# The output bias of an expert block: three pieces held in 3 rows, or in 128 rows of which 125 are zero

## The chip, the cores and the metric

The kernel runs on one core of a Trainium2 chip. The metric is the device time of one execution, in microseconds. The time before is 408.74 us, the median of three runs (407.4 to 409.92). Of the core's engines TensorE is called PE, VectorE DVE, ScalarE ACT, GpSimd POOL and SyncE SP. PE loads a stationary operand (a weight load, PEld in the profile) and then streams a moving operand through it (a matmul).

## What is computed

Sixteen sequences of 256 tokens with 128 features go through one layer: a layer norm, a causal linear attention with a residual, a second layer norm, and a mixture of 8 experts, of which each token takes the best two. Cut to what matters here:

```
x = x + attention(layernorm(x))
logits = layernorm(x) @ Wr + br                 # top 2 of 8 experts per token
h = relu(layernorm(x) @ W1[e] + b1[e])          # 128 -> 512
expert_out = h @ W2[e] + b2[e]                  # 512 -> 128, the bias b2 is the subject here
x = x + sum over the token's 2 experts of routed * expert_out
```

## The kernel before

**Stages.** Projections for the attention run until about 50 us, the attention with its prefix sums and the routing of tokens until about 240 us. During the routing POOL writes each token's normalised row to a table in HBM, `x_rows`, at a place that belongs to its expert (indirect DMAs, L468, two for each tile of 128 tokens). Then comes the stage of the experts: `NBLK` = 39 blocks of 256 places (`GPB` = 2 tiles of 128), each of one expert. Their results go back to `y_rows` in HBM by POOL's indirect DMAs (`scatter_y`, L500 to L506, two for a block). After the last one SP loads `y_rows`, ACT and DVE mix it into `x`, and SP stores the output.

**A block of experts.** The order is written out by hand, engine by engine (L1390 to L1395 for PE): at step n PE does `up(n+2)`, `down(n)`, `turn_block(n+4)`.
- `turn_block` (L1324): 4 matmuls of 128 columns turn the loaded rows around.
- `up` (L1342 to L1344): 12 matmuls of 256 columns, in fp16. Ahead of them PE's sequencer loads the block's expert number (L1332).
- `down`: first the matmul with the bias (L1364), 256 columns, then 16 matmuls of 128 columns (L1372, L1373) and 8 more (L1377), in fp16. Of the first 16, half use registers that the sequencer computes from the expert number just ahead of them.

**Around PE.** ACT copies the turned rows (L654), applies bias and relu (L669), and copies a block's result out of PSUM (L677) into one of 8 buffers (`YG`), from which POOL scatters it. DVE rounds the hidden values to fp16 (the cast, L1058) and makes the rest (L1062, a subtraction), one of each for a block. POOL's order, too, is by hand: two x scatters and then the two y scatters of block n for n = 0 to 5 (L515 to L518), then y scatters alone. SP loads block n's rows (L352). From block `N1` = 15 on this waits for all x scatters; its turn stands on PE after `down(11)`.

**The bias.** `b2` is split into three bf16 pieces, whose sum is the fp32 value. Each piece is a row of `b2p` (3 partitions, 8 experts x 128). The matmul at L1364 has `ones3` (3 x 128, all one) as its stationary operand and the expert's three rows of `b2p` as moving operand, so that it writes the sum of the pieces to every token's row. `ones3` is set by POOL at L395, `b2p` comes by a DMA of SP at L337. A second tile, `ones_b` (96 rows of ones, bf16, L373), is the stationary operand of the two bias matmuls of the projections (L1142, L1144).

Of the kernel before, what the change touches and what calls it, by code (L numbers as in the profile page):

```python
# [7 lines left out]
BF16 = mybir.dt.bfloat16  # L8
# [6 lines left out]
def block_kernel(nc, x_d, wqkv_d, bqkv_d, wproj_d, bproj_d, w1_d, b1_d, w2_d, b2_d, wr_d, br_d, out_d):  # L15

    P = 128
    SEQS, T, D = x_d.shape
    NT = SEQS * T // P
    U = SEQS  # L20
    TPU = T // P
    H, DH = 16, D // 16
    E, _, HID = w1_d.shape
    HC = HID // P
    LN_EPS, DEN_EPS = 1e-5, 1e-6
# [13 lines left out]
    B_ROWS = 96  # L39
# [3 lines left out]
    GPB = 2  # L43
# [34 lines left out]
    b2_parts = nc.dram_tensor("b2_parts", [3, E, D], BF16).ap()  # L78
    yv = y_rows[0:YROWS, :].rearrange("(p t c) d -> p t c d", p=P, c=TOP)

    with ExitStack() as ctx:
        def sb(name, shape, dt=F32):
            return ctx.enter_context(nc.sbuf_tensor(name, shape, dt))

        def sem(name):
            return ctx.enter_context(nc.semaphore(name))

        ps = ctx.enter_context(nc.psum_tensor("ps", [P, 8, 512], F32))
# [17 lines left out]
        bias_qk = sb("bias_qk", [B_ROWS, TPU, 2 * D], BF16)  # L106
        bias_v = sb("bias_v", [B_ROWS, TPU, D], BF16)
        bproj = sb("bproj", [P, D])
        ones_b = sb("ones_b", [B_ROWS, P], BF16)

        b1r = sb("b1r", [E * HC, P])
        b1T = sb("b1T", [P, E * HC])
        b1s = sb("b1s", [P, E * HC])
        b2hml = sb("b2hml", [E, 3, D], BF16)
        b2p = sb("b2p", [3, E, D], BF16)
        ones3 = sb("ones3", [3, P], BF16)
        ident = sb("ident", [P, P])
        tri = sb("tri", [P, P])
        ones = sb("ones", [P, P])
# [94 lines left out]
        late_done = sem("late_done")  # L214
# [28 lines left out]
        b2_in = sem("b2_in")  # L243
# [78 lines left out]
        @block.sync  # L322
        def _(sp):
            for g in range(LOADS):
                gt = slice(LN_TILES[g], LN_TILES[g + 1])
                sp.dma_start(x[:, gt, :], xv[:, gt, :]).then_inc(x_in[g], 16)
            sp.dma_start(wf[:, 0, :].rearrange("p (e h) -> p e h", e=E), w1_d.rearrange("e d h -> d e h")).then_inc(w1_in, 16)
            sp.dma_start(wf[:, 1, :].rearrange("p (e c d) -> p e c d", e=E, c=HC),
                         w2_d.rearrange("e (c p) d -> p e c d", p=P)).then_inc(w2_in, 16)
            sp.wait_ge(empty_done, 1)  # L330
            for e in range(E + 1):
                sp.dma_start(x_rows[e * REGION:e * REGION + SLOTS, :].rearrange("(p g) w -> p g w", g=GPB),
                             empty[:, :, :]).then_inc(empty_out, 16)
            sp.wait_ge(b2_done, 1)
            sp.dma_start(b2_parts.rearrange("r e d -> e r d"), b2hml[:, :, :]).then_inc(b2_in, 16)
            sp.wait_ge(b2_in, 16)
            sp.dma_start(b2p[:, :, :], b2_parts).then_inc(b2_in, 16)  # L337

            regs = [sp.alloc_register(name=f"row{j}") for j in range(XG)]
            for n in range(NBLK):  # L340
                b = n % XG
                if n in (0, N1):
                    i = 0 if n == 0 else 1
                    sp.wait_ge(table_done, 2 * (i + 1))
                    for c in range(TOP):
                        sp.wait_ge(x_scattered[i][c], 16 * (NT - T1 if i else T1))
                sp.load(regs[b:b + 1], table_i[0:1, 0, n:n + 1])
                row = sp.snap(regs[b], min_val=0, max_val=E * REGION)
                if n >= XG:
                    sp.wait_ge(turn_done, n - XG + 1)  # L350
                    sp.wait_ge(yid_done, n - XG + 1)
                sp.dma_start(xg_w[:, b, :], x_rows[bass.ds(row, SLOTS), :].rearrange("(p g) w -> p (g w)", g=GPB)  # L352
                             ).then_inc(loaded[b], 16)

            for b in range(YG):
                sp.wait_ge(y_scattered[b], 16 * GPB * len(range(b, NBLK, YG)))
            for g in range(Y_LOADS):
                gt = slice(g * TPY, (g + 1) * TPY)
                sp.dma_start(yg[:, gt], yv[:, gt]).then_inc(y_in[g], 16)
            for g in range(Y_LOADS):  # L360
                gt = slice(g * TPY, (g + 1) * TPY)
                sp.wait_ge(mix_done, g + 1)
                sp.dma_start(ov[:, gt, :], x[:, gt, :]).then_inc(out_done, 16)
            sp.wait_ge(out_done, 16 * Y_LOADS)

        @block.gpsimd
        def _(pool):
# [24 lines left out]
            layer_norm_1(1)  # L392
            layer_norm_1(2)
            nc.gpsimd.memset(empty[:, :, :], 0.0).then_inc(empty_done, 1)
            nc.gpsimd.memset(ones3[:], 1.0).then_inc(late_done, 1)  # L395
            nc.gpsimd.memset(ones_h[:], 1.0).then_inc(late_done, 1)
            nc.gpsimd.memset(picked[:, 0, :], 0.0).then_inc(late_done, 1)
            nc.gpsimd.iota(ints[:, 0:E], [[1, E]], base=0, channel_multiplier=0).then_inc(late_done, 1)
# [721 lines left out]
        def _(pe):  # L1120
# [15 lines left out]
            def qkv(u):  # L1136
                par = u % 2
                pe.wait_ge(xT_out, u + 1)
                if u >= 2:
                    pe.wait_ge(phi_done, u - 1)  # L1140
                    pe.wait_ge(v_done, u - 1)
                nc.tensor.matmul(ps[:, 2 + par, :], ones_b[:, :], bias_qk[:, :, :].rearrange("p a d -> p (a d)"),  # L1142
                                 start=True, stop=False)
                nc.tensor.matmul(ps[:, 4 + par, 0:T], ones_b[:, :], bias_v[:, :, :].rearrange("p a d -> p (a d)"),  # L1144
                                 start=True, stop=False)
                for a in range(TPU):
                    xT = xT_s[:, par, a * P:(a + 1) * P]
                    nc.tensor.matmul(ps[:, 2 + par, a * 2 * D:(a + 1) * 2 * D], xT, wqkv[:, 0:2 * D],  # L1148
                                     start=False, stop=(a == TPU - 1))
                    ins = nc.tensor.matmul(ps[:, 4 + par, a * D:(a + 1) * D], xT, wqkv[:, 2 * D:3 * D],  # L1150
                                           start=False, stop=(a == TPU - 1))
                ins.then_inc(qkv_done, 1)
# [140 lines left out]
            def spread(i):  # L1293

                n = (N1, N2)[i]
                pe.wait_ge(diag_done, 5 * (i + 1))
                nc.tensor.matmul(ps[:, 5 + i, (0, T)[i]:(0, T)[i] + 5 * n].rearrange("p (k n) -> p k n", k=5),
                                 ones[:, :], diag[:, :, 0:n], start=True, stop=True).then_inc(spread_done, 1)
# [49 lines left out]
            def down(n):  # L1348
                e = pe.snap(regs[n % 4], min_val=0, max_val=E - 1)
                if n >= 2:  # L1350
                    pe.wait_ge(y_out, n - 1)
                if n == 0:
                    pe.wait_ge(cnt_out, 2)
                if n == 1:
                    pe.wait_ge(rank_out, NG)
                if n == SPREAD - 1:
                    pe.wait_ge(y_out, n)
                if n == SPREAD:
                    pe.wait_ge(y_out, n)
                    spread(1)  # L1360
                if n == SPREAD + 2:
                    pe.wait_ge(table_done, 4)
                both = ps[:, 6 + n % 2, 0:GPB * D].rearrange("p (g d) -> p g d", g=GPB)
                nc.tensor.matmul(both, ones3[:, :], b2p[:, bass.ds(e, 1), :].broadcast_to([3, GPB, D]), start=True, stop=False)  # L1364
                outs = [ps[:, 6 + n % 2, g * D:(g + 1) * D] for g in range(GPB)]
                high = [(w2[:, bass.ds(e, 1), c, 0].rearrange("p a d -> p (a d)")) for c in range(HC)]
                low = [(w2[:, bass.ds(e, 1), c, 1].rearrange("p a d -> p (a d)")) for c in range(HC)]
                pe.wait_ge(hi_done, n + 1)
                for g, o in enumerate(outs):
                    for c in range(HC):  # L1370
                        h = hh[:, n % 2, c, g * P:(g + 1) * P]
                        nc.tensor.matmul(o, h, high[c], start=False, stop=False)  # L1372
                        nc.tensor.matmul(o, h, low[c], start=False, stop=False)  # L1373
                pe.wait_ge(lo_done, n + 1)
                for g, o in enumerate(outs):
                    for c in range(HC):
                        ins = nc.tensor.matmul(o, hl[:, n % 2, c, g * P:(g + 1) * P], high[c], start=False,  # L1377
                                               stop=(g == GPB - 1 and c == HC - 1))
                ins.then_inc(down_done, 1)
# [10 lines left out]
            for n in range(NBLK):  # L1390
                if n + 2 < NBLK:
                    up(n + 2)
                down(n)
                if n + 4 < NBLK:
                    turn_block(n + 4)  # L1395
# [23 lines left out]
```

## Time and profile before

| | |
|---|---|
| median of three runs | 408.74 us (407.4 to 409.92) |
| the profiled execution, its time | 409.99 us |
| its span, first to last instruction | 408.2 us |
| PE busy | 311.4 us, 2455 matmuls |
| PE weight loads | 240.3 us |
| DVE busy | 295.6 us |
| POOL busy | 279.7 us |
| ACT busy | 192.9 us |
| mean granted clock of PE | 0.889 |

The profiled execution took 1.8 us more than its span. Busy shares are means over stages that have different limits. A matmul's recorded time includes its way through the array, so matmuls that follow each other overlap in the records: what one costs is the distance from its start to the next start. In the timeline a number in brackets is the idle time of the engine before the row, with what ended it. "issue" means that nothing in the profile ended it.

### The profile page before, as it was taken

Reading aid. Unit: us, or ns where it says so; the run is one execution under the profiler, and the core shown is the slowest. Engines: PE = TensorE matmul, PEld = TensorE weight load, DVE = VectorE, ACT = ScalarE, POOL = GpSimd, SP = SyncE. Lnnn points to the kernel's source line nnn. Section 1 sums busy time; section 2 is a strip of 40 time slices with the busy share of each in tenths; the row PEclk is TensorE's granted clock in tenths of the full one; section 3 lists DMA queues with packets and bytes.
Section 4 is the critical chain, followed back from the end, with each engine's and each line's share of the span. In section 5 each row is a group of like instructions: output and inputs, shape, how many; then the busy total and the mean of one; then the engine's idle time right before and its main releaser. Section 6 shows DMA issues by size and latency. Waiting matters only on the chain.

```text
span 408.2 us, 8336 instructions
## 1 busy us (share of the span) xinstructions
PE 311.4 (76%) x2455; PEld 240.3 (59%) x2455; DVE 295.6 (72%) x707; ACT 192.9 (47%) x479; POOL 279.7 (69%) x249
## 2 busy tenths in 40 slices
PE   0799696986899895898942479999899999993000
PEld 0578464664676663575731347888788888883000
DVE  3988948777789899698993577777567776673067
ACT  2498306277521510513130436766677777762063
POOL 3479525899945888898667463788778788787600
PEclk9999988898999998998975559999999999999555
DMA  7990000000000000000011042221423322111198
GB/s 206 321 256 3 1 2 1 1 2 0 0 2 0 28 28 26 26 26 29 33 46 54 20 125 67 82 73 44 137 84 96 85 82 81 57 43 47 51 359 259
DMA packets 24064, 29.41 MB, mean 72 GB/s; under 512 B 3819, under 2 KB 18675, under 8 KB 24022
## 3 DMA queue, kind: packets, MB, share of 16 engines
q1 hardware_dynamic: 18582, 18.99, 15.5%
q0 software_dynamic: 4544, 9.38, 7.2%
q10 hardware_dynamic: 896, 0.50, 0.5%
q8 instruction: 23, 0.38, 0.4%
q14 instruction: 19, 0.16, 0.1%
HBM read 16.19 MB, written 12.67 MB: 71 GB/s over the span
## 4 chain that ended last, share of the span: by engine, by line
PE 28%; DVE 24%; issue 20%; POOL 14%; ACT 6%; DMA 5%; SPq 1%; POOLq 0%; DVEq 0%; ACTq 0%
POOL y_rows L504 12%; PE ps L1175 7%; DVE work L839 5%; DVE nd L845 4%; PE ps L1174 2%; DVE y_s L856 2%; DMA qk<-y_rows 2%; PE ps L1148 2%; DVE wm L747 2%; ACT xs L603 2%; POOL x_rows L468 2%; PE ps L1342 2%; PE ps L1343 2%; PE ps L1344 2%; PE ps L1372 2%
## 5 line engine op out<-in xcount | busy, mean ns | idle before, releaser
L504 POOL DMA_INDIRECT y_rows<-kvt,yid x78 | 95.4, 1223 | 30.4 <-issue 21.6
L438 POOL TENSOR_TENSOR kvt<-qk,v 128x1024 f32<-128x1024 f32 x32 | 67.5, 2133 | 29.7 <-PE ps L1179 18.9
L468 POOL DMA_INDIRECT x_rows<-rows,pos_i x64 | 66.0, 1031 | 30.5 <-issue 17.3
L1175 PE MATMUL ps<-kvt,tri 128*128 128x384 f32 (+1 forms) x192 | 72.9, 493 | 11.6 <-DVE work L839 11.6
L669 ACT ACTIVATE wraw<-ps,b1s 128x256 f32<-128x256 f32 x156 | 61.1, 474 | 3.1 <-PE ps L1344 2.5
L1175 PEld LDWEIGHTS ps<-kvt,tri 128*128 128x128 f32 x192 | 38.3, 206 | 33.2 <-issue 18.0
L1058 DVE CAST wraw<-wraw 128x1024 f16<-128x1024 f32 x39 | 27.3, 699 | 34.5 <-ACT wraw L669 33.3
L839 DVE TENSOR_TENSOR work<-ps,qk 128x1152 f32<-128x1152 f32 x32 | 42.2, 1350 | 11.0 <-PE ps L1179 10.7
L1062 DVE TENSOR_TENSOR wraw<-wraw 128x1024 f16<-128x1024 f32 x39 | 47.8, 1225 | 1.3
L1342 PE MATMUL ps<-wraw,w1h 128*128 128x256 f16 x156 | 43.7, 280 | 0.3 <-issue 0.3
L1343 PE MATMUL ps<-wraw,w1h 128*128 128x256 f16 x156 | 43.7, 280 | 0.0
L1344 PE MATMUL ps<-wraw,w1l 128*128 128x256 f16 x156 | 43.6, 279 | 0.0
L845 DVE TENSOR_REDUCE nd<-work 128x144 f32<-128x1152 f32 x32 | 41.6, 1341 | 0.0
L1372 PE MATMUL ps<-w,wraw 128*128 x312 | 40.6, 221 | 0.8 <-DVE wraw L1058 0.8
L1373 PE MATMUL ps<-w,wraw 128*128 x312 | 40.1, 219 | 0.0
L1174 PE MATMUL ps<-kvt,ones 128*128 128x384 f32 (+1 forms) x96 | 37.0, 467 | 0.0
L1372 PEld LDWEIGHTS ps<-w,wraw 128*128 128x128 f16 x312 | 29.5, 97 | 6.0 <-issue 1.3
L677 ACT ACTIVATE kvt<-ps 128x256 f32<-128x256 f32 x39 | 14.9, 383 | 35.3 <-PE ps L1377 35.3
L1373 PEld LDWEIGHTS ps<-w,wraw 128*128 128x128 f16 x312 | 30.4, 98 | 0.4
L654 ACT ACTIVATE wraw<-ps 128x512 f16<-128x512 f32 x39 | 23.1, 594 | 5.1 <-PE ps L1324 5.1
L588 ACT ACTIVATE xT_s<-ps 128x256 f32<-128x256 f32 x16 | 6.1, 383 | 40.3 <-PE ps L1186 40.3
L1377 PE MATMUL ps<-w,wraw 128*128 x312 | 23.8, 219 | 0.0
(211 smaller groups left out, 643.1 us busy)
## 6 DMA issues: line engine op xcount, KB each, us to landing
wraw<-x_rows SPq DMA_DIRECT2D x39, 130.0 KB, 2.3
qk<-y_rows SPq DMA_DIRECT2D x8, 512.0 KB, 6.5
wraw<-in_L_ffn_W_dram SPq DMA_DIRECT2D x1, 2048.0 KB, 12.7
out_dram<-x SPq DMA_DIRECT2D x8, 256.0 KB, 4.7
x<-in_L_attn_x_dram SPq DMA_DIRECT2D x3, 512.0 KB, 10.0
y_rows<-kvt,yid POOLq DMA_INDIRECT x78, 2.5
x_rows<-empty SPq DMA_DIRECT2D x9, 130.0 KB, 4.1
x_rows<-rows,pos_i POOLq DMA_INDIRECT x64, 2.3
```

What stands on the lines that cost most here:

```text
L438: nc.gpsimd.tensor_tensor(kvt[:, u % RING, a].rearrange("p (j h i) -> p j h i", j=DH, i=DH), k.unsqueeze(1).broadcast_to([P, DH, H, DH]), ...
L468: nc.gpsimd.indirect_dma_start(out=x_rows, out_offset=bass.IndirectOffsetOnAxis(ap=pos_i[:, c, t:t + 1], axis=0), in_=rows[:, t, :], in_of ...
L504: nc.gpsimd.indirect_dma_start(out=y_rows, in_=ysb[:, n % YG, g], in_offset=None, out_offset=bass.IndirectOffsetOnAxis(ap=yid[:, n, g:g + ...
L669: ins = nc.scalar.activation(hid[:, n % 2, c], ps[:, 2 + 2 * (n % 2) + c // 2, at:at + SLOTS], ACT.Relu, bias=b1s[:, bass.ds(e * HC + c, 1)])
L839: nc.vector.tensor_tensor(m_s[:, a].rearrange("p (b j n) -> p b j n", b=3, j=PLB), ps[:, 3 * a:3 * a + 3, 0:PLB * D].rearrange("p b (j n) ...
L845: nc.vector.tensor_reduce(nd[:, s % 2, a, :], m_s[:, a].rearrange("p (n i) -> p n i", i=DH), AX.X, ALU.add).then_inc(red_done, 1)
L1175: nc.tensor.matmul(o, tri[:, :], kv[a][:, cols], start=(a == 0), stop=True)
L1342: nc.tensor.matmul(o, wh, xh, start=True, stop=False)
L1343: nc.tensor.matmul(o, wh, xl, start=False, stop=False)
L1344: ins = nc.tensor.matmul(o, wl, xh, start=False, stop=True)
L1372: nc.tensor.matmul(o, h, high[c], start=False, stop=False)
L1373: nc.tensor.matmul(o, h, low[c], start=False, stop=False)
```

## The change

`ones_b` has 128 rows instead of 96. `ones3` is gone. `b2p` has 128 rows: POOL clears it, where it set `ones3` before, and SP's DMA then writes the pieces into rows 0 to 2, behind a wait for POOL's late constants. The bias matmul of a block takes all 128 rows of `ones_b` and of `b2p`. The bias matmuls of the projections take the first 96 rows of `ones_b`, as before.

```
-        ones_b = sb("ones_b", [B_ROWS, P], BF16)
+        ones_b = sb("ones_b", [P, P], BF16)
...
-        b2p = sb("b2p", [3, E, D], BF16)
-        ones3 = sb("ones3", [3, P], BF16)
+        b2p = sb("b2p", [P, E, D], BF16)
...
             sp.wait_ge(b2_in, 16)
-            sp.dma_start(b2p[:, :, :], b2_parts).then_inc(b2_in, 16)
+            sp.wait_ge(late_done, 16)
+            sp.dma_start(b2p[0:3, :, :], b2_parts).then_inc(b2_in, 16)
...
-            nc.gpsimd.memset(ones3[:], 1.0).then_inc(late_done, 1)
+            nc.gpsimd.memset(b2p[:, :, :], 0.0).then_inc(late_done, 1)
...
-                nc.tensor.matmul(both, ones3[:, :], b2p[:, bass.ds(e, 1), :].broadcast_to([3, GPB, D]), start=True, stop=False)
+                nc.tensor.matmul(both, ones_b[:, :], b2p[:, bass.ds(e, 1), :].broadcast_to([P, GPB, D]), start=True, stop=False)
```

No instruction is added, removed or moved on PE, ACT, DVE or SP. On POOL the order is the same as well, and two fills have another size. This is POOL's list at the constants that are set after the first layer norms; `empty` is the block of zeros with which `x_rows` is cleared.

```order
 L394 MEMSET empty 128x260
-L395 MEMSET ones 3x128
+L395 MEMSET b2p 128x1024
 L396 MEMSET ones_h 128x128
 L397 MEMSET picked 128x8
```

The fill at L395 has grown from 128 to 1024 elements in a partition, and stays in its place.

## Rows read from the trace of the kernel before

**Rows 1.** The page, chain of work that ended last, by line.
```profile
POOL y_rows L504 12%; PE ps L1175 7%; DVE work L839 5%; DVE nd L845 4%; PE ps L1174 2%; DVE y_s L856 2%; DMA qk<-y_rows 2%; PE ps L1148 2%; DVE wm L747 2%; ACT xs L603 2%; POOL x_rows L468 2%; PE ps L1342 2%; PE ps L1343 2%; PE ps L1344 2%; PE ps L1372 2%
```

**Rows 2.** Windows: stretch, length, busy us of PE, PEld, DVE, ACT, POOL, then clock.
```profile
310.00:362.00 52.00, 52.00 (x667) 44.82 (x665) 36.60 (x67) 38.12 (x99) 41.94 (x34) 1.00 0.26 75
362.00:386.00 24.00, 9.38 (x116) 7.42 (x114) 7.44 (x16) 6.24 (x17) 18.69 (x18) 0.79 0.15 47
```

**Rows 3.** Timeline of PE: start, duration, line, operation, tiles.
```profile
320.55 0.27 PE L1343 MATMUL ps<-wraw,w1h 128*128 128x256 f16 x1
320.66 0.27 PE L1344 MATMUL ps<-wraw,w1l 128*128 128x256 f16 x1
320.87 0.28 PE L1364 MATMUL ps<-b2p,ones 3*128 x1
321.08 0.23 PE L1372 MATMUL ps<-w,wraw 128*128 x1
321.14 0.22 PE L1373 MATMUL ps<-w,wraw 128*128 x1
```

**Rows 4.** Timeline of the weight loads (PEld), the same place.
```profile
320.86 0.09 PEld L1364 LDWEIGHTS ps<-b2p,ones 3*128 3x128 bf16 x1 [0.21 <-issue]
```

**Rows 5.** Line L1364 from 308 to 362: count, ns, first and last start; idle before.
```profile
L1364 PE MATMUL ps<-b2p,ones x17: 278/278/279, 308.1 to 359.1; 3*128 x17
...
  issue: 3.6, 17
```

**Rows 6.** Timeline of PE in the projections: 96 rows, bf16, then fp32.
```profile
17.71 0.27 PE L1144 MATMUL ps<-bias_v,ones_b 96*128 96x256 bf16 x1
17.82 0.60 PE L1148 MATMUL ps<-wqkv,xT_s 128*128 128x256 f32 x2
```

**Rows 7.** Timeline of PE in the routing: one row, then 128 rows, both fp16.
```profile
246.47 0.18 PE L1249 MATMUL ps<-base_h,ones_h 1*128 1x16 f16 x1
246.58 0.18 PE L1250 MATMUL ps<-picked,before_h 128*128 128x16 f16 x1
```

**Rows 8.** Line L1332 of PE's sequencer, from 286 to 290, and from 287 to 360.
```profile
L1332 PEldq TENSOR_LOAD <-table_i x2: 297/302/307, 286.9 to 289.8; - x2
...
L1332 PEldq TENSOR_LOAD <-table_i x24: 297/300/355, 286.9 to 359.9; - x24
```

**Rows 9.** Timelines of DVE and of POOL, a block in the middle.
```profile
324.99 0.69 DVE L1058 CAST wraw<-wraw 128x1024 f16<-128x1024 f32 x1 [0.91 <-ACT wraw L669]
325.72 1.23 DVE L1062 TENSOR_TENSOR wraw<-wraw 128x1024 f16<-128x1024 f32 x1
...
326.15 1.62 POOL L504 DMA_INDIRECT y_rows<-kvt,yid  x1 [0.31 <-issue]
328.08 0.96 POOL L504 DMA_INDIRECT y_rows<-kvt,yid  x1 [0.30 <-issue]
```

**Rows 10.** Timelines of DVE and of POOL, near the end of the blocks.
```profile
366.24 0.69 DVE L1058 CAST wraw<-wraw 128x1024 f16<-128x1024 f32 x1 [0.41 <-ACT wraw L669]
...
366.63 1.12 POOL L504 DMA_INDIRECT y_rows<-kvt,yid  x1 [0.30 <-issue]
```

**Rows 11.** Timeline of PE, the turn of block 15.
```profile
286.85 0.40 PE L1324 MATMUL ps<-ident_h,wraw 128*128 128x128 f16 x4 [1.19 <-DMA wraw<-x_rows]
```

**Rows 12.** Timeline of POOL, its last scatter.
```profile
384.91 0.96 POOL L504 DMA_INDIRECT y_rows<-kvt,yid  x1 [0.31 <-issue]
```

**Rows 13.** Timeline of POOL, two fills.
```profile
1.34 0.53 POOL L374 MEMSET bias_qk<- 96x512 bf16 x1
...
19.18 0.19 POOL L395 MEMSET ones<- 3x128 bf16 x1
```

**Rows 14.** Timelines of POOL and ACT, behind the constants.
```profile
24.36 0.20 POOL L389 TENSOR_TENSOR shift<-lnt,rstd 128x8 f32<-128x8 f32 x1
26.25 0.87 ACT L538 ACTIVATE work<-x,shift,rstd 128x128 f32<-128x128 f32 x2
28.78 1.66 POOL L387 TENSOR_TENSOR rstd<-lnt,neghalf 128x8 f32<-128x8 f32 x1 [1.89 <-DVE lnt L722]
```

More of the change, by code:

```diff
@@ L1141, in qkv @@
                     pe.wait_ge(v_done, u - 1)
-                nc.tensor.matmul(ps[:, 2 + par, :], ones_b[:, :], bias_qk[:, :, :].rearrange("p a d -> p (a d)"),
+                nc.tensor.matmul(ps[:, 2 + par, :], ones_b[0:B_ROWS, :], bias_qk[:, :, :].rearrange("p a d -> p (a d)"),
                                  start=True, stop=False)
-                nc.tensor.matmul(ps[:, 4 + par, 0:T], ones_b[:, :], bias_v[:, :, :].rearrange("p a d -> p (a d)"),
+                nc.tensor.matmul(ps[:, 4 + par, 0:T], ones_b[0:B_ROWS, :], bias_v[:, :, :].rearrange("p a d -> p (a d)"),
                                  start=True, stop=False)
```

## The prediction

> **What bounds the kernel now.** I read the chain that ended last first. Its largest entry is POOL's scatter of results, L504, with 12% of the span [rows 1]. Then I read the windows, to see which engine is full beside POOL: from 310 to 362 us PE is busy for all of 52.00 us, POOL for 41.94, ACT for 38.12 and DVE for 36.60 [rows 2]. So two engines could be the bound of the expert blocks: PE, which never rests, and POOL, which still has work when PE has none. In the next window PE is busy for 9.38 us and POOL for 18.69 [rows 2], and the last scatter starts at 384.91 [rows 12]. All that follows (loads, mixing, stores) hangs on that scatter. The reader should keep both in mind: a faster PE is worth something only if POOL becomes faster with it.
>
> The period of a block is (359.1 - 308.1) / 16 = 3.19 us [rows 5]. The sequencer's line gives the same over a longer stretch: (359.9 - 286.9) / 23 = 3.17 [rows 8].
>
> **What the bias matmul costs.** Two up matmuls of 256 columns start 0.11 us apart (320.55, 320.66). The bias matmul starts 0.21 after the last of them, and the first down matmul 0.21 after the bias (320.87, 321.08) [rows 3]. It has 256 columns as well, so that a matmul like its neighbours would take 0.11 on each side. The surplus is 0.10 + 0.10 = 0.20 us for a block. The weight load of the bias sits idle for 0.21 us ahead of it, with nothing in the profile that ended it [rows 4], and this is so at all 17 blocks of the stretch, 3.6 us in all [rows 5]; elsewhere in that window loads run beside matmuls (44.82 us of them under 52.00 us [rows 2]).
>
> Is it the three rows, or the bf16 among fp16? Two places tell them apart. In the projections a bias matmul of 96 rows in bf16 with 256 columns is followed by an fp32 matmul after 17.82 - 17.71 = 0.11 us [rows 6]: another type, many rows, no surplus. In the routing a matmul of one row and only 16 columns is followed by one of 128 rows, both fp16, after 0.11 us [rows 7], twice the 0.06 that separates two down matmuls of 128 columns [rows 3]: one type, few rows, and a surplus. So it goes with the rows. I expect 0.20 us less for a block; the bounds are 0 (the gaps stay) and 0.20 (nothing can be closer than its neighbours).
>
> A rule of the Trainium skill names such a mechanism: "TensorEngine Tiling (Array Packing)", section Tiling Modes, Key Properties, says that going from one tiling mode to another makes the array drain, and rows 3 fit it on both sides of the bias. By that rule the whole 0.20 us goes. A second page speaks against the change: "TensorE: Matmul & The Clock Gate", Part 3, has a weight load overlap matmuls in flight only where it targets another row group, which padding to 128 rows would take away. Rows 4 disagree: the small load is the one that doesn't overlap.
>
> **Does the sequencer keep up?** PE's period would be 3.19 - 0.20 = 2.99. Its sequencer also computes registers and loads an expert number. Right behind the stall of block 15 its queue is empty, and there it went from one block's load to the next in 289.8 - 286.9 = 2.9 us [rows 8]. That is one sample, read to a tenth. It is close enough to 2.99 that some blocks may be held up by it, so the gain per block is between 0.18 and 0.20, with 0.10 as a poor case.
>
> **Does POOL follow?** In steady state POOL does two scatters for a block: one of 1.62 and one of 0.96 us, each after 0.30 of idle: 1.62 + 0.96 + 0.60 = 3.18, PE's period [rows 9]. Alone they would take 2 x (0.96 + 0.30) = 2.52. The 0.66 us of the long one is either a fixed price of working beside DVE, or a wait for DVE. Its end tells: DVE's subtraction ends at 325.72 + 1.23 = 326.95, and the long scatter at 326.15 + 1.62 = 327.77, 0.82 later [rows 9]. Near the end, at another phase, a scatter is stretched by only 0.16 (1.12 instead of 0.96); DVE's cast ends at 366.24 + 0.69 = 366.93, and this scatter at 366.63 + 1.12 = 367.75, again 0.82 later [rows 10]. So a scatter that starts under one of DVE's two long operations waits for its end, and then takes 0.82. POOL is held in step by DVE, DVE by ACT, ACT by PE. DVE and ACT have room (36.60 and 38.12 of 52.00 [rows 2]).
>
> At a period of 2.99, measured from the end of the subtraction: scatter one ends at 0.82, scatter two starts at 1.12 (0.30 of idle). The cast now begins 2.99 - (0.69 + 1.23 + 0.04) = 1.03 and ends at 1.72; scatter two waits for it and ends at 2.54; scatter three starts at 2.84, under the subtraction, which ends at 2.99. The pattern closes, two scatters to a block, at any period above 2.52. So POOL's stretch shrinks by what PE's period does, and its backlog behind PE at the end stays as it is.
>
> **The other edits.** POOL's fill of 128 rows x 1024 bf16 in place of 3 x 128: 96 x 512 took 0.53, 3 x 128 took 0.19 [rows 13], (0.53 - 0.19) / (512 - 128) x (1024 - 128) = 0.8 us more; the bounds are 0 and twice that. It delays what stands behind it on POOL. The shift of the fourth group ends at 24.36 + 0.20 = 24.56 and ACT uses it at 26.25, 1.7 us later; before the fifth POOL waits 1.89 us for DVE [rows 14]. Both cover 0.8; without that cover it would be 0.8 us once. SP's new wait needs POOL's late constants, which DVE has waited for too (L915) before it made the pieces that this DMA carries: nothing. `ones_b` with 128 rows instead of 96 has the same elements in a partition: nothing.
>
> **The sum.** Blocks 0 to 11 gain 0.20 each on PE. Then PE waits 1.19 us for the load of block 15 [rows 11], which hangs on the last x scatter. POOL reaches that scatter in step with DVE, over some ten periods, so it comes about 10 x 0.20 = 2.0 us earlier, and the wait stays. Behind it blocks 12 to 36 gain 25 x 0.20 = 5.0. The last two blocks are bound by latencies. That is 7.0 us with 0.20, and 6.3 with 0.18. POOL may fall a step out of phase once, which costs up to one stretch of 0.66. I take 6.5 us. The profiled span would go from 408.2 to 401.7, its time from 409.99 to 403.5; the median of runs lay 1.25 below that execution, so the median goes from 408.74 to 402.2.
>
> **Rivals.**
> - *Both follow* (0.74): 402.2, its own range 401 to 403.8.
> - *Half of it* (0.08): only one of the two gaps closes, or the sequencer holds PE at about 3.09. 35 x 0.10 = 3.5 us, 405.2. For it: one sequencer sample near the limit. Against: the registers of L1364 are no more than before.
> - *POOL doesn't follow* (0.11): the 0.66 is a fixed price, or the gaps stay (the change does nothing, 0.03 of this). POOL needs 3.18 for a block as before, PE only gets further ahead until the 8 buffers are full: 408.7. Against it is the stretch of 0.16 in rows 10.
> - *Slower* (0.07): POOL's phase turns bad. If the cast falls on the middle of a scatter and the subtraction on the start of the next, both are stretched; taken as 0.16 more for the second than now [rows 10], over 35 blocks that is 5.6 us, 414.3, and with a full 0.66 twice it would be 23 us. It decides where the cast starts after scatter two has begun: 1.12 after the subtraction's end, that is at a period above 1.12 + 1.96 = 3.08; at today's 3.19 it starts 0.11 after, and its end just clears the end of the scatter. The shorter period moves away from that, hence the small chance.
> - Among the slower ones, 0.02: a load of 128 rows that has to wait for the matmuls ahead lies open with 0.09 us [rows 4] in 39 blocks, 3.5 us: 412.2. This is what the second page would make of it.
>
> **How the numbers follow.** About 1% (4.1 us) is what can be told from no change here, so faster means under 404.6. The first case lies wholly there: 0.74, and a part of the second, where the sequencer costs less than half, brings it to 0.76. The same: the rest of the second and the third, 0.17. Slower: 0.07. For eight in ten the range takes in the first case and the second: 400.6 (the full 7.0 us and 1.1 of scatter between medians) to 405.6.
>
> **What the new profile would show.** The bias matmul starts 0.11 after the last up matmul, and the first down matmul 0.11 after it; no idle time ahead of the load of L1364; a period of 2.99 to 3.01. POOL's scatters of a block take 0.96 and about 1.42, or two stretched ones with 0.46 between them. The wait before block 15's turn is still about 1.2. The last scatter starts near 378.4. If the gaps are gone and the last scatter still starts near 385, the step about POOL is wrong; if the gaps are there, the step about rows.

## The result and the profile after

The changed kernel takes 403.32 us (median of five runs, 401.13 to 406.1) where the kernel before takes 408.74 (five runs, 406.69 to 411.76). The ratio is 0.986, with an interval of 0.9814 to 0.9905: 5.4 us faster. The prediction was 402.2, with a range of 400.6 to 405.6.

| | before | after |
|---|---|---|
| median | 408.74 us | 403.32 us |
| profiled execution, its time | 409.99 us | 406.1 us |
| its span | 408.2 us | 404.3 us |
| PE weight loads, busy | 240.3 us | 245.7 us |
| POOL busy | 279.7 us | 275.6 us |
| L504, mean of a scatter | 1223 ns | 1169 ns |
| mean granted clock | 0.889 | 0.891 |

The profiled execution of after is the slowest of its five, so its span must be read with care. Below, the lengths of its stages are compared with those of before, and not only its end.

PE around the bias matmul, the place of [rows 3], as the timeline of after has it:

```profile
320.95 0.27 PE L1344 MATMUL ps<-wraw,w1l 128*128 128x256 f16 x1
321.06 0.27 PE L1364 MATMUL ps<-b2p,ones_b 128*128 x1
321.17 0.22 PE L1372 MATMUL ps<-w,wraw 128*128 x1
```

The bias matmul starts 0.11 us after the up matmul, and the first down matmul 0.11 after the bias. Both gaps of 0.21 are gone. The line L1364 over the window from 305 to 360 answers to [rows 5]:

```profile
L1364 PEld LDWEIGHTS ps<-b2p,ones_b x18: 97/98/98, 305.8 to 357.4; 128*128 128x128 bf16 x18
L1364 PE MATMUL ps<-b2p,ones_b x18: 272/272/273, 305.9 to 357.6; 128*128 x18
```

The 3.6 us of idle time ahead of its weight load, "issue", no longer stand there. The period is (357.6 - 305.9) / 17 = 3.04 us, where it was 3.19.

The windows of after (start and end, length, busy us of PE, PEld, DVE, ACT, POOL, then the granted clock, the DMA share and GB/s), the first two for [rows 2]:

```profile
310.00:362.00 52.00, 52.00 (x707) 48.91 (x705) 38.02 (x69) 39.90 (x103) 41.63 (x35) 1.00 0.27 80
362.00:386.00 24.00, 7.49 (x92) 6.22 (x89) 7.04 (x13) 4.68 (x13) 15.43 (x15) 0.75 0.21 65
...
251.90:380.80 128.90, 115.34 (x1517) 107.06 (x1514) 84.80 (x165) 86.12 (x222) 102.32 (x88) 0.96 0.26 77
```

In the same 52 us PE does 707 matmuls where it did 667. The third window is the most telling. It runs from POOL's first scatter of results to its last one. The same stretch of before is this:

```profile
250.90:384.90 134.00, 119.03 (x1517) 101.55 (x1514) 84.78 (x166) 86.30 (x222) 107.43 (x87) 0.97 0.25 74
```

DVE and ACT have the same busy time in both. POOL is busy for 107.43 us of 134.00 before, and for 102.32 of 128.90 after. What is left is 26.57 and 26.58: POOL has about 88 scatters in either window and idles 0.30 us ahead of each. In neither trace is any idle time ahead of a scatter in these windows longer than 0.31 us. So POOL works through the whole stage without a break in both kernels, and all of the 5.1 us comes out of the recorded duration of its scatters. None comes from idle waits. (A scatter's duration contains what it waits for DVE, as the part on why the prediction was right shows.)

### The profile page after: what moved, and what is told of

Read it like the earlier page. It is cut to its first block, busy times and chain, and to the rows that moved or that the text cites. A ratio compares the mean times of both kernels' runs of the same rounds, so it can differ in the third digit from the quotient of the medians.

```text
span 404.3 us, 8337 instructions
## 1 busy us (share of the span) xinstructions
PE 307.2 (76%) x2455; PEld 245.7 (61%) x2455; DVE 297.3 (74%) x707; ACT 192.9 (48%) x479; POOL 275.6 (68%) x249
## 4 chain that ended last, share of the span: by engine, by line
DVE 27%; POOL 22%; PE 20%; issue 16%; ACT 7%; DMA 5%; SPq 1%; POOLq 0%; ACTq 0%; DVEq 0%
POOL y_rows L504 18%; PE ps L1175 6%; DVE work L839 5%; DVE nd L845 4%; POOL x_rows L468 4%; DVE y_s L856 3%; DMA qk<-y_rows 3%; PE ps L1174 3%; PE ps L1148 2%; DVE wm L747 2%; ACT xs L603 2%; DMA x<-in_L_attn_x_dram 1%; DVE qk L742 1%; PE ps L1150 1%; DVE rd L853 1%
## 5 line engine op out<-in xcount | busy, mean ns | idle before, releaser
L504 POOL DMA_INDIRECT y_rows<-kvt,yid x78 | 91.2, 1169 | 30.3 <-issue 20.1
L1372 PE MATMUL ps<-w,wraw 128*128 x312 | 43.5, 222 | 1.1 <-DVE wraw L1058 1.0
L1373 PE MATMUL ps<-w,wraw 128*128 x312 | 43.3, 223 | 0.0
L1372 PEld LDWEIGHTS ps<-w,wraw 128*128 128x128 f16 x312 | 30.9, 99 | 2.7 <-issue 1.6
L1373 PEld LDWEIGHTS ps<-w,wraw 128*128 128x128 f16 x312 | 30.1, 99 | 1.9
L1377 PE MATMUL ps<-w,wraw 128*128 x312 | 24.0, 220 | 0.0
```

What stands on the lines that cost most here:

```text
L504: nc.gpsimd.indirect_dma_start(out=y_rows, in_=ysb[:, n % YG, g], in_offset=None, out_offset=bass.IndirectOffsetOnAxis(ap=yid[:, n, g:g + ...
```

## Experiments

Each experiment was made on one chip together with runs of the kernel before. There were four such sets. In two of them the kernel before took 408.92 and 408.59 us, as it did when its profile was taken; in the other two it took 424.32 and 428.37. Those two sets are read by themselves.

### Is it the rows, and from what size on?

Four kernels keep everything of the change (the larger fill, SP's wait, `ones_b`, the 128 rows of `b2p`) and give the matmul at L1364 fewer of the rows: 3, 32, 64 or 96. The rows left out are zero, so the result is the same.

```
-  matmul(both, ones_b[:, :], b2p[:, bass.ds(e, 1), :].broadcast_to([P, GPB, D]), ...)
+  matmul(both, ones_b[0:3, :], b2p[0:3, bass.ds(e, 1), :].broadcast_to([3, GPB, D]), ...)
```

> The changed kernel with the bias matmul of a block back on 3 rows of ones_b and 3 rows of b2p; the wider tiles, POOL's larger fill and SP's added wait stay. Theory (a matmul of few rows between matmuls of 128 rows costs about 0.10 us on each side, and nothing else in the change matters): the gaps of 0.21 us before and behind L1364 are back, the period is 3.19 us, the time is that of the kernel before, 408.7 us, ratio 0.997 to 1.003. Rival (part of the 5.4 us came from elsewhere, as from the layout of the tiles): under 407 us. Rival (the larger fill and the wait cost something): over 409.5 us.

> The bias matmul of a block with 32 rows, all zero but the three pieces. Theory 1 (the array has modes of 32, 64 and 128 rows, and going between them costs): as with 3 rows, first down matmul 0.21 us behind the bias, period 3.19. Theory 2 (the surplus grows smaller with each row that is added): gaps between 0.11 and 0.21.

> The bias matmul of a block with 64 rows. Theory 1 (modes of 32, 64 and 128 rows): 64 rows is another mode than 128, the gaps stay at 0.21 us and the period at 3.19. Theory 2 (only matmuls that fit into 32 rows are special): 0.11 us and a period of about 3.04.

> The bias matmul of a block with 96 rows, as the bias matmuls of the projections have. Theory 1 and 2 alike: 0.11 us on both sides and a period of 3.04, as with 128 rows, since 96 rows need all of the array's rows. If gaps are left, then it is not modes, and all 128 rows are needed.

The line L1364 in the window from 305 to 360, of the kernels with 3, 32, 64 and 96 rows (the idle time ahead of its weight load is shown for the first; with 96 rows there is none):

```profile
L1364 PE MATMUL ps<-b2p,ones_b x17: 278/278/278, 306.5 to 357.5; 3*128 x17
...
  issue: 3.6, 17
```

```profile
L1364 PE MATMUL ps<-b2p,ones_b x18: 278/278/279, 305.1 to 359.3; 32*128 x18
```

```profile
L1364 PE MATMUL ps<-b2p,ones_b x17: 279/279/280, 306.9 to 358.0; 64*128 x17
```

```profile
L1364 PE MATMUL ps<-b2p,ones_b x19: 274/274/275, 305.2 to 359.8; 96*128 x19
```

| rows of L1364 | gap ahead, behind | period | span | time |
|---|---|---|---|---|
| 3 | 0.20, 0.21 | 3.19 | 406.8 | 409.11, 10 runs, ratio to before 0.9999 (0.9968 to 1.0031) |
| 32 | 0.20, 0.21 | 3.19 | 409.4 | 411.28, one run |
| 64 | 0.20, 0.21 | 3.19 | 407.1 | 408.92, one run |
| 96 | 0.11, 0.11 | 3.03 | 403.4 | 405.21, one run |
| 128 (after) | 0.11, 0.11 | 3.04 | 404.3 (that execution took 406.1) | 403.32, median of five |

The periods are worked out as above, for 96 rows (359.8 - 305.2) / 18. The edge lies between 64 and 96 rows: with 3, 32 and 64 rows the price is the same, so it doesn't shrink with each row that is added. With 64 rows, half of the 128, the timeline shows both gaps:

```profile
322.66 0.27 PE L1344 MATMUL ps<-wraw,w1l 128*128 128x256 f16 x1
322.86 0.28 PE L1364 MATMUL ps<-b2p,ones_b 64*128 x1
323.07 0.23 PE L1372 MATMUL ps<-w,wraw 128*128 x1
```

The kernel with 3 rows has the whole of the change but this one number, and has the time of before. So the gain of the kernel after hangs on the rows of the matmul alone, and the larger fill and SP's wait cost nothing that shows. All five kernels have bf16 beside fp16, so the type alone makes no gap. The times of the single runs are worth less than the periods: where the stage of experts starts differs between executions. ACT's copy of block 0 starts at 250.6, 249.1 and 250.7 us with 32, 64 and 96 rows.

### Is the price one for a matmul, or for a change of size?

The kernel before, with its bias matmul issued twice in a row (the second adds the bias again).

```
   matmul(both, ones3[:, :], b2p[:, bass.ds(e, 1), :].broadcast_to([3, GPB, D]), start=True, stop=False)
+  matmul(both, ones3[:, :], b2p[:, bass.ds(e, 1), :].broadcast_to([3, GPB, D]), start=False, stop=False)
```

> The kernel before with the bias matmul of 3 rows issued twice in a row (the bias is added twice, so the output differs by b2). If the price is for each change between few rows and 128 rows: the second matmul starts 0.11 us behind the first, and the surplus of a block stays 0.20: 0.21 ahead, 0.11 between, 0.21 behind, a period of 3.30. If each matmul of few rows is slow by itself: 0.21 between the two, and a period of 3.40. The second matmul also needs a register, 0.12 us of the sequencer, which had room before.

```profile
331.38 0.27 PE L1344 MATMUL ps<-wraw,w1l 128*128 128x256 f16 x1
331.59 0.28 PE L1364 MATMUL ps<-b2p,ones 3*128 x1
331.71 0.27 PE L1365 MATMUL ps<-b2p,ones 3*128 x1
331.91 0.23 PE L1373 MATMUL ps<-w,wraw 128*128 x1
```

The distances are 0.21, 0.12 and 0.20. Between the two small matmuls there is nearly no surplus (0.12 where neighbours of 256 columns are 0.11 apart); it stands once on the way in and once on the way out. The period of 3.30 that was expected couldn't be tested, and the time of this run (425.60 us) says nothing, since its chip was one of those with another bound.

### Does the sequencer hold PE up?

The prediction had PE's period at 2.99 if only PE counts, and after shows 3.04. The timeline of after shows where the rest is. These are down matmuls of one block, all of 128 columns:

```profile
315.39 0.22 PE L1373 MATMUL ps<-w,wraw 128*128 x1
315.46 0.23 PE L1372 MATMUL ps<-w,wraw 128*128 x1
315.58 0.23 PE L1373 MATMUL ps<-w,wraw 128*128 x1
315.65 0.22 PE L1372 MATMUL ps<-w,wraw 128*128 x1
```

They start 0.06 us apart, but one comes after 0.12. From 310 to 357 us after has 9 such distances over 0.1 among the first 16 down matmuls of its blocks, and what these matmuls have above 0.056 adds up to 0.88 us, or 0.06 for each of some 15 blocks. A block without any takes 2.98 us, and 2.98 + 0.06 is the period of 3.04. Before has no distance over 0.1 there, nor has the kernel with 3 rows. All nine are ahead of the eighth of the 16, the last one whose register the sequencer computes just ahead. In the trace of after its computations for L1372 and L1373 (FUSED_REGOPS) start 0.124 us apart, as the two matmuls above do (315.46, 315.58), while PE by itself needs 0.056 for such a matmul. So the trace alone speaks for the sequencer; three experiments were to test it. The first lets the sequencer load two experts' numbers with one instruction, in every other block.

```
-                pe.load(regs[n % 4:n % 4 + 1], table_i[0:1, 1, n:n + 1])
+                at = (n + 1) % 4
+                if n == 0:
+                    pe.load(regs[at:at + 1], table_i[0:1, 1, n:n + 1])
+                elif n % 2 == 1:
+                    pe.load(regs[at:at + 2], table_i[0:1, 1, n:n + 2])
```

> The changed kernel, in which PE's sequencer loads the expert numbers of two blocks with one load (blocks 1 and 2, 3 and 4, and so on). A load and its wait took 0.36 us in the trace of after, so this frees 0.18 us of the sequencer for a block. Theory (the 0.05 us by which the period of after, 3.04, is over the 2.99 that PE's own matmuls need is the sequencer's): the period from block 16 on falls to 2.99 to 3.00, some 1.0 to 1.8 us off the time before x 0.987, about 401.8 us. Rival (the 0.05 is something else, as DVE or ACT): the period stays at 3.04 and the time at 403.3.

> The changed kernel with one load of expert numbers for two blocks, once more, since the first look ran on a chip on which the kernel before took 424 us and the blocks had another bound. If this chip takes 409 us for the kernel before: by the theory of the sequencer the period from block 16 on is 2.99 to 3.00 instead of 3.04, and the time about 402 us; by the rival 3.04 and 403.3. A load of two numbers took 0.60 us with its wait on the other chip instead of 0.36, so a block frees 0.06 us rather than 0.18, which just covers the 0.05. If it is a chip of 424 us again: as the kernel before.

On the chip where before took 424.32 this kernel took 424.53, a ratio of 0.9982 (0.9947 to 1.0017), no difference. On the chip where before took 408.59 it took 406.06 (ten runs), a ratio of 0.9957 (0.9929 to 0.9986): a little faster than before, yet behind the plain change (0.986, and 403.18 below on this same chip). Neither forecast came true, 402 us with a period of 2.99 or 403.3 with 3.04: the period from 310.5 to 354.3 us is 43.8 / 14 = 3.13. ACT's copies of the results show how it runs:

```profile
309.17 0.39 ACT L677 ACTIVATE kvt<-ps 128x256 f32<-128x256 f32 x1 [0.36 <-PE ps L1381]
312.45 0.38 ACT L677 ACTIVATE kvt<-ps 128x256 f32<-128x256 f32 x1 [0.94 <-PE ps L1381]
315.43 0.39 ACT L677 ACTIVATE kvt<-ps 128x256 f32<-128x256 f32 x1 [0.64 <-PE ps L1381]
318.78 0.38 ACT L677 ACTIVATE kvt<-ps 128x256 f32<-128x256 f32 x1 [1.02 <-PE ps L1381]
```

The steps are 3.28, 2.98 and 3.35 us. A block without a load takes the 2.98 that PE alone allows, and one with the load of two takes 0.3 more. Where the 0.3 lies is seen in a block with the load, in its fourth to eighth down matmul:

```profile
310.78 0.22 PE L1377 MATMUL ps<-w,wraw 128*128 x1
310.89 0.23 PE L1376 MATMUL ps<-w,wraw 128*128 x1
311.04 0.23 PE L1377 MATMUL ps<-w,wraw 128*128 x1
311.17 0.23 PE L1376 MATMUL ps<-w,wraw 128*128 x1
311.29 0.23 PE L1377 MATMUL ps<-w,wraw 128*128 x1
```

```profile
L1336 PEldq TENSOR_LOAD <-table_i x9: 538/602/678, 308.2 to 358.3; - x9
```

The load of two takes 602 ns (median) where a load of one takes 302 in after, and behind it the matmuls come at the sequencer's 0.12 us, not at PE's 0.06. In the blocks without a load all 15 distances are 0.056. So it is the sequencer's work that keeps after above 2.98, and to bunch this work makes it worse: what one block saves, PE can't use below 2.98, and what the other has more, it pays.

The second lets the bias matmul always take expert 0, so that it needs no register.

```
-  matmul(both, ones_b[:, :], b2p[:, bass.ds(e, 1), :].broadcast_to([P, GPB, D]), ...)
+  matmul(both, ones_b[:, :], b2p[:, 0:1, :].broadcast_to([P, GPB, D]), ...)
```

> The changed kernel with the bias of expert 0 for every block, so that L1364 needs no register (the output's bias is wrong for the other experts; this is what is left out). The sequencer has 0.12 us less to do for a block. Theory of the sequencer: period 2.99 to 3.00 instead of 3.04. Rival: 3.04.

> The changed kernel with the bias of expert 0 for every block (left out: the choice of the bias by expert, so the output differs by biases), again for a chip on which the kernel before takes 409 us. L1364 then needs no register, 0.12 us less for the sequencer in a block, and unlike with one load for two blocks the work is less in every block. By the theory of the sequencer the period falls from 3.04 to 2.99 or 3.00, PE's own pace, and the distance between blocks is the same from one to the next within 0.02. By the rival it stays at 3.04.

It gave 421.11 us where before took 424.32, and 427.12 where before took 428.37. Both chips were of the kind with another bound. Its period in the first was (363.8 - 307.1) / 16 = 3.54 us, so it says nothing on the sequencer at 3.0. Whether one register less in every block would bring 2.99 stays open.

The third was to add a second load to each block, on top of after and of before.

```
-            regs = [pe.alloc_register(name=f"pe_expert{b}") for b in range(4)]
+            regs = [pe.alloc_register(name=f"pe_expert{b}") for b in range(5)]
...
+                pe.load(regs[4:5], table_i[0:1, 1, n:n + 1])
```

> The changed kernel with one more load of the expert number by PE's sequencer in each block, into a register that nothing uses: 0.36 us more of the sequencer, nothing more of PE. Theory of the sequencer: period 3.04 + 0.36 = 3.40. Rival (the sequencer has room): 3.04 to 3.1.

> The kernel before with the same extra load. Theory of the sequencer: before the change it had 3.19 - 3.02 = about 0.17 us of room in a block, so the period goes to 3.38 to 3.40, where extra stands too: with a slower sequencer the change would bring nothing. Rival (the sequencer has room): 3.19 to 3.25.

> The changed kernel with one more load of the expert number in each block, again for a chip on which the kernel before takes 409 us. By the theory of the sequencer the period is 3.40, 0.36 more than after, and some 11 us are lost against it. By the rival (room in the sequencer) 3.04 to 3.1. On a chip of 424 us: no difference from the kernel before, as in the first look.

This test was void, and its forecasts (a period of about 3.40) stay untested. Nothing uses the fifth register, and the built program has 39 loads, as before:

```profile
L1333 PEldq TENSOR_LOAD <-table_i x39: 295/301/491, 239.6 to 385.2; - x39
```

So these kernels are the plain after, twice, and the plain before. As that they were of use. `extra_again` took 403.18 us, with a span of 401.3: after once more, on a chip of the usual kind.

### Where the gain goes: PE's stall and POOL's line

With it there are two executions of the same program to hold against each other. In the one of after, PE's wait for the last x rows [rows 11] is longer, and something follows it:

```profile
287.19 0.40 PE L1324 MATMUL ps<-ident_h,wraw 128*128 128x128 f16 x4 [2.00 <-DMA wraw<-x_rows]
...
289.05 0.42 PE L1342 MATMUL ps<-wraw,w1h 128*128 128x256 f16 x1
```

```profile
287.00:291.00 4.00, 3.55 (x28) 2.93 (x29) 1.20 (x2) 2.12 (x5) 3.09 (x4) 0.70 0.71 201
291.00:295.00 4.00, 4.00 (x53) 3.85 (x52) 1.20 (x4) 2.33 (x6) 3.09 (x4) 0.87 0.33 103
```

After 2.00 us of waiting the granted clock falls to its lower level, 1.2 GHz: matmuls of 256 columns take 0.42 us, and the windows show 0.70 and 0.87 of the clock. That costs PE (0.30 + 0.13) x 4 = 1.7 us. The kernel with 96 rows has the same: a wait of 2.07 us, then 0.61 from 287 to 291. In before and in `extra_again` the waits were 1.19 and 1.39 us, and the clock stayed at 1.00. ACT's copy of block 12 comes 41.2 us after its copy of block 0 in after (251.30, 292.45), and 39.2 in `extra_again` (248.04, 287.20). So PE is 2 us late in after, at the same program. But POOL's stretch from its first scatter of results to its last is no longer. These are windows of `extra_again` and of the kernel with 96 rows:

```profile
248.60:378.10 129.50, 114.03 (x1517) 105.88 (x1515) 85.11 (x165) 86.15 (x222) 102.88 (x88) 0.96 0.27 77
```

```profile
251.30:380.10 128.80, 115.10 (x1517) 106.80 (x1514) 84.97 (x165) 86.30 (x222) 102.20 (x88) 0.96 0.27 77
```

The stretch takes 129.50 us with PE on time, and 128.90 and 128.80 with PE late by 2. What shrinks is POOL's backlog: from ACT's last copy to POOL's last scatter it is 12.70 us in before and in `extra_again`, and 10.17 in after. So a late PE costs nothing here, as POOL still has scatters to do. That it even helps a little, because a DVE that rests doesn't stretch scatters, would fit the 0.6 us, but three executions don't show it. The kernels with 3 rows and with paired loads have the same rest:

```profile
249.30:383.40 134.10, 118.94 (x1516) 101.47 (x1514) 84.77 (x166) 86.38 (x222) 107.56 (x88) 0.97 0.26 74
```

```profile
251.10:383.30 132.20, 117.61 (x1517) 107.28 (x1514) 84.69 (x164) 86.45 (x222) 105.63 (x88) 0.96 0.26 75
```

Length less POOL's busy time is 26.6 in all of them: 134.10 - 107.56 = 26.54, 132.20 - 105.63 = 26.57, 129.50 - 102.88 = 26.62. The stage is as long as POOL's scatters with their idle time of 0.30 are. PE's rest is no constant: length less PE's busy time is 13.6 in after and 15.5 in `extra_again`.

### Two chips with another bound

In two of the four sets the kernel before took 424 and 428 us. In the first of these sets plain after and plain before were there beside each other, one run each: 424.02 and 423.01. The gaps at the bias matmul are as elsewhere (before has 3.2 us of "issue" ahead of 15 weight loads), but the period isn't set by them. It is (363.0 - 313.3) / 14 = 3.55 us with 128 rows and (362.0 - 312.1) / 14 = 3.56 with 3. Of plain before on that chip, a window, the largest waits of the experts' stage, and ACT at the end of a block:

```profile
310.00:362.00 52.00, 50.68 (x597) 40.59 (x594) 32.65 (x58) 33.49 (x88) 31.86 (x29) 1.00 0.28 79
```

```profile
ACT kvt L677 <- PE ps L1378: 42.7, 34, 2.6
POOL y_rows L504 <- ACT kvt L677: 36.1, 31, 2.1
```

```profile
333.12 0.38 ACT L677 ACTIVATE kvt<-ps 128x256 f32<-128x256 f32 x1 [1.24 <-PE ps L1378]
```

POOL has next to no backlog there (1.9 us at the end of the stage, against 12.7). It waits for ACT's copy, and ACT's copy starts about 1.2 us after the recorded end of the last down matmul, where on the other chips it starts within 0.1. The semaphore events of this trace show that it isn't ACT that is late: PE's signal for this matmul is recorded at 333.10, while the matmul's own record ends at 331.88. In all six traces of these chips the signal lags by 1.2 to 1.4 us (median of the blocks), in the others by 0.01. In the window above the granted clock is 1.00, as elsewhere.

The late signal isn't the whole difference, though. The first 12 blocks take 55.9 us here (from copy to copy) and 40.4 in before. Early in the stage PE stands still 16 times with "issue" as the only reason, for 8.8 us in all, where before has one such stop of 0.26, and the granted clock is at its lower level for 10 us:

```profile
261.50:271.70 10.20, 6.39 (x41) 4.19 (x39) 4.63 (x9) 3.54 (x10) 6.55 (x7) 0.50 0.19 52
```

These traces also hold a third fewer semaphore events (3468 against 5120), so something beside the kernel differs. What it is was not found, whether the recording itself has a part in it is not known, and nothing was tried on it.

## Why the prediction was right, and where it was off

**The rows.** Right in kind and in size: 0.10 us on each side, with the rows and not with the type. What was inferred from the 96 bf16 rows of the projections [rows 6], the kernel with 96 rows shows directly. The rule of the Trainium skill, "TensorEngine Tiling (Array Packing)", section Tiling Modes, Key Properties, that a change of tiling mode makes the array drain, fits what was measured: 64 rows and fewer pay on the way in and out, 96 and 128 don't, and two small matmuls in a row pay once. The cause inside the array was not seen. The objection from the Trainium skill, "TensorE: Matmul & The Clock Gate", Part 3, that a weight load overlaps matmuls in flight only where its row group differs, is not borne out: the load of L1364 now has 128 rows and runs beside the matmul ahead of it, with no idle time.

**The sequencer.** The prediction was right that the sequencer comes near, and made its cost too small. It took a gain of 0.18 to 0.20 for a block, so at most 0.02 for the sequencer, from one sample of 2.9 us between two loads [rows 8]. Measured are 3.19 - 3.04 = 0.15: PE's own gain is 3.19 - 2.98 = 0.21, and the sequencer takes 0.06 of it. The terms that were mis-sized are 10 x 0.20 and 25 x 0.20: one sample, taken after a stall, stood for a pace that varies between blocks.

**POOL follows.** Right, with the numbers of the model. POOL and DVE in the middle of after:

```profile
346.46 1.42 POOL L504 DMA_INDIRECT y_rows<-kvt,yid  x1 [0.30 <-issue]
348.19 0.95 POOL L504 DMA_INDIRECT y_rows<-kvt,yid  x1 [0.30 <-issue]
...
346.36 0.69 DVE L1058 CAST wraw<-wraw 128x1024 f16<-128x1024 f32 x1 [0.71 <-ACT wraw L669]
347.09 1.22 DVE L1062 TENSOR_TENSOR wraw<-wraw 128x1024 f16<-128x1024 f32 x1
```

The scatters take 1.42 and 0.95, as forecast for a period of 2.99. The cast ends at 347.05 and the scatter that started under it at 347.88, the subtraction at 348.31 and the other scatter at 349.14: 0.83 after, both times. It is so throughout: of the 63 scatters of after that start while one of these two operations runs, 58 end 0.82 to 0.84 us after its end, and of 43 in before 42 do. The exceptions all start within 0.04 us of a cast's start; they take 0.95 to 0.97, and it is the cast that takes longer (0.74 to 0.76). POOL's backlog behind ACT's last copy is 12.70 us in before and in the repeat of after, so it stayed as it was where PE wasn't held up more. So the rival in which the 0.66 is a fixed price is out, and so are the slower ones.

**The stall in between.** Here the prediction was wrong in its numbers, and it didn't matter. It had the last x scatter 2.0 us earlier and PE's wait unchanged at 1.2. Counted from the copy of block 0, the last x scatter starts at 31.36 in before (250.30, 281.66) and at 30.16 in after (251.30, 281.46), 1.2 us earlier. The wait was 2.00 in after and 1.39 in its repeat. That PE then lost 1.7 us more to the clock was in no step. None of it reached the end, since POOL has a backlog there: from ACT's first copy to its last, PE's side of the stage got only 2.6 us shorter in after (121.91, 119.27), and POOL's 5.2.

**The fills.** The new fill took 0.96 us where the old one took 0.19, 0.77 more (0.8 was expected), and POOL still waits for DVE in the fifth group:

```profile
18.82 0.96 POOL L395 MEMSET b2p<- 128x1024 bf16 x1
...
28.87 1.66 POOL L387 TENSOR_TENSOR rstd<-lnt,neghalf 128x8 f32<-128x8 f32 x1 [1.59 <-DVE lnt L722]
```

**The sum.** The prediction took 6.5 us; the medians give 5.4. The stage, from the copy of block 0 to the last scatter, went from 134.61 us (250.30 to 384.91) to 129.44 in after (251.30 to 380.74) and 130.02 in its repeat (248.04 to 378.06): 5.2 and 4.6 us. With 0.15 in place of 0.20 the prediction's own 35 blocks give 5.3. The last scatter of after's profiled execution starts at 380.74 and not at 378.4, of which 1.0 us is that its stage began later. Where it begins differs between executions by 3.3 us even for the same program (251.30 and 248.04), and that is all of the 2.9 us between their times (406.1, 403.18). The other executions of after, from 401.13 us on, have no trace. So that the median came within 1.1 us of the forecast is in part luck: the stage itself gained 5.2 and 4.6 us where 6.5 were forecast.

The sum was built on the wrong engine, though. It counted what PE gains block by block and then asked whether POOL follows. In blocks without a stall the two give the same, but stalls tell them apart: a stall of PE is no loss while POOL has a backlog. Had it been built on POOL, it would have read: 88 scatters of 0.96 + 0.30 us, and for each block that DVE works through, a stretch of the period less 2.52. With the prediction's 35 blocks that estimate gives 110.9 + 35 x 0.67 = 134.3 us before and 110.9 + 35 x 0.52 = 129.1 after, where 134.0 and 128.8 were measured from the first scatter's start to the last one's.

## What to carry to other kernels

A bf16 matmul with 3, 32 or 64 rows between fp16 matmuls of 128 rows cost 0.20 us here, beyond its columns. The same matmul padded with zero rows to 96 or 128 cost nothing more than its columns. Two small ones in a row paid once. So pad such matmuls, or put them together. Before counting on the gain, look for what comes next: the pace of the sequencer took a quarter of it, and the rest reached the end only because the engine with the backlog is held in step by the ones that became faster. To find the engine that works through a stage without a break, take its busy time over the stage from several kernels: here the length less POOL's busy time was the same in all of them. That tells which engine the stage is as long as; what lengthens its instructions, here DVE's two operations, has to be read from their ends.

## What was not expected of the hardware

- The edge between paying and not paying is between 64 and 96 rows, and there is no slope on either side of it: 3, 32 and 64 rows all cost 0.20 us, 96 and 128 nothing.
- Waits of 2.00 and 2.07 us on PE were followed by a lower clock (0.70 and 0.61 in the next window of 4 us), waits of 1.19 and 1.39 us by none. The same program had a wait of 2.00 in one execution and of 1.39 in another, so the difference doesn't come from the change alone.
- A scatter of POOL that starts under one of DVE's two long operations ends 0.83 us after that operation's end, whatever their phase; one that starts together with a cast isn't held up.
- On two of the chips the same kernel before took 424 to 428 us instead of 409, with PE's signal for a block's result 1.2 us late and a first stretch of the stage 15 us longer, and there the change brought nothing that could be told.
